# Routed rows fetched by indirect transfers instead of gathered on TensorE, and x added by VectorE instead of by an accumulating transfer

## The reference: what is computed

```
xn = layernorm(x)
s  = causal_attention(xn)                        # one head of width 256
for each token: two experts of eight are picked, with weights w (softmax, bias, groups)
flat_idx = the picked expert numbers themselves  # values 0 to 7
routed_in = xn[flat_idx] * w                     # so only tokens 0 to 7 are ever read
h   = silu(routed_in @ w1[e]) * (routed_in @ w3[e]) ; routed_out = h @ w2[e]
out = shared_ffn(xn); out[flat_idx] += routed_out    # only tokens 0 to 7 are written
x  + s * silu(out)
```

## Time and profile before

| what | value |
|---|---|
| time, median of 3 runs | 243.1 us (241.94 to 243.17) |
| time of the profiled execution | 242.11 us |
| span of the profiled execution | 240.4 us |
| mean granted TensorE clock | 0.999 of full speed |
| busy | PE 96%, DVE 74%, ACT 60%, POOL 24% |
| transfers | 19.45 MB, 81 GB/s over the span |

### The profile page before, as it was taken

The page is one execution under the profiler, slowest core; times in us unless marked ns, Lnnn a source line. Parts: engine busy times, 40 slices in busy tenths (PEclk is TensorE's granted clock), DMA queues, the critical chain, the costliest instruction groups (busy, mean ns, idle before and its releaser), DMA issues.

```text
span 240.4 us, 4667 instructions
## 1 busy us (share of the span) xinstructions
PE 230.6 (96%) x1553; PEld 204.5 (85%) x1553; DVE 177.1 (74%) x580; ACT 145.3 (60%) x390; POOL 57.5 (24%) x108
## 2 busy tenths in 40 slices
PE   6799999999999999999999999999999999999991
PEld 4789898998988989889899998898988879899760
DVE  3489658887987898878767976668586777769635
ACT  2445655755648557465575643877869686788711
POOL 3320721815508236072011000002020120202022
PEclk9999999999999999999999999999999999999999
DMA  6599420020200200000000000110845638375465
GB/s 183 189 323 307 138 87 3 5 84 4 87 4 0 87 3 1 1 3 0 0 3 0 1 3 3 48 40 11 203 73 155 115 108 169 78 189 86 140 121 180
DMA packets 18726, 19.45 MB, mean 81 GB/s; under 512 B 1032, under 2 KB 17680, under 8 KB 18704
## 3 DMA queue, kind: packets, MB, share of 16 engines
q1 hardware_dynamic: 15008, 15.50, 20.3%
q0 software_dynamic: 3696, 3.67, 10.0%
HBM read 14.95 MB, written 4.21 MB: 80 GB/s over the span
## 4 chain that ended last, share of the span: by engine, by line
PE 90%; DVE 4%; issue 1%; DMA 1%; ACT 1%; POOL 1%; DVEq 0%; ACTq 0%
PE bank L390 82%; PE bank L479 4%; PE bank L440 3%; DMA x_ring<-in_L_attn_x 1%; PE bank L412 1%; DVE x_ring L1349 1%; PE bank L431 1%; DVE bn L945 1%; DVE w L1343 1%; PE bank L547 1%; DVE xT_lo_all L936 1%; POOL rstd L307 0%; DVE arena L936 0%; DVE w L1265 0%; ACT w L885 0%
## 5 line engine op out<-in xcount | busy, mean ns | idle before, releaser
L390 PE MATMUL bank<-xT_hi_all,arena 128*128 128x512 f32 (+3 forms) x256 | 80.3, 369 | 0.0
L390 PE MATMUL bank<-arena 128*128 128x256 f32 (+2 forms) x560 | 75.9, 282 | 0.4 <-ACT attn_all L723 0.3
L390 PEld LDWEIGHTS bank<-arena 128*128 128x128 f32 (+1 forms) x560 | 71.0, 183 | 5.3 <-DVE arena L936 1.1
L723 ACT ACTIVATE arena<-bank 128x512 fp32r<-128x512 f32 (+4 forms) x84 | 36.3, 452 | 28.9 <-PE bank L390 27.4
L390 PEld LDWEIGHTS bank<-xT_hi_all,arena 128*128 128x128 f32 x256 | 47.0, 189 | 6.1 <-DVE arena L936 0.2
L936 DVE TENSOR_TENSOR arena<-bank,arena 128x264 fp32r<-128x264 f32 (+4 forms) x83 | 41.3, 507 | 14.3 <-ACT arena L723 14.1
L390 PE MATMUL bank<-xT_lo_all,arena 128*128 128x512 f32 (+3 forms) x128 | 45.8, 358 | 0.0
L376 POOL DMA_DIRECT2D x_ring<-in_L_attn_x x7 | 9.2, 1311 | 88.8 <-DVE x_ring L1284 88.8
L390 PEld LDWEIGHTS bank<-xT_lo_all,arena 128*128 128x128 f32 x128 | 24.2, 189 | 2.1
L723 ACT ACTIVATE attn_all<-bank,row_inv 128x256 f32<-128x256 f32 x32 | 15.2, 475 | 15.6 <-PE bank L390 14.7
L747 ACT ACTIVATE probs<-bank,neg_max 128x128 f32<-128x128 f32 (+3 forms) x32 | 17.0, 531 | 9.4 <-DVE neg_max L985 9.4
(11 more groups left out here) (125 smaller groups left out, 376.4 us busy)
## 6 DMA issues: line engine op xcount, KB each, us to landing
x_ring<-in_L_attn_x SPq DMA_DIRECT2D x8, 512.0 KB, 3.4
x_ring<-in_L_attn_x POOLq DMA_DIRECT2D x7, 512.0 KB, 5.8
out<-x_ring SPq DMA_DIRECT2D x7, 512.0 KB, 3.4
spread<-pairs SPq DMA_DIRECT2D x14, 128.0 KB, 3.4
w_sb<-in_L_ffn_w SPq DMA_DIRECT2D x1, 1024.0 KB, 10.9
raw_sw<-in_L_ffn_sw SPq DMA_DIRECT2D x3, 256.0 KB, 4.3
x_ring<-in_L_attn_x SPq DMA_DIRECT2D x2, 256.0 KB, 3.0
raw_qkv<-in_L_attn_WQ SPq DMA_DIRECT2D x1, 256.0 KB, 4.1
```

Of the source, the lines that this page charges most:

```text
L390: return nc.tensor.matmul(dst, lhsT, rhs, start=start, stop=stop, skip_group_check=True, **kw)
L723: return nc.scalar.activation(dst, src, ACT.Copy, scale=scale)
```

## The change

- Groups 1 to 7 (56 of the 64 tiles) no longer use `gather` and `one_hot`. The table A is written to DRAM once (64 rows of 512 bytes), and POOL issues 56 indirect transfers (`fetch_rows`), each of which fetches 128 rows of A by index into the SBUF space of `xn`. `silu_rows` reads from there. A group's buffer is fetched anew as soon as ACT has read it.
- The pair numbers' way through DRAM goes: `turn_pairs`, the ACT copy to `pair_T`, the store, and the 14 `spread` loads.
- x is loaded again by SP for all 8 batches (`reload_x`) into `x_ring`; the gate goes into `gate` instead, and DVE adds x in halves (`add_x`, 14 instructions). The 7 accumulating transfers on POOL go. `store` waits for its own landing before the next load.
- Added once: a copy of A and a transpose of it (`A_full`, `A_rows`), and the conversion of the pair numbers into indices (`pair_ids`).

```diff
 # SP
-            def load_pairs(i):
...
+            def reload_x(i):
+                sp.wait_ge(s["x_loaded"], 16 * (B + i - 1))
+                load_x(sequence(i), i)
             def store(i):
-                sp.wait_ge(s[f"summed{i % 2}"], 16 * (i // 2 + 1))
+                sp.wait_ge(s["summed"], 2 * (i + 1))
                 sp.dma_start(out_v[sequence(i), :, :, :], x_ring[:, i % 2, :, :]).then_inc(s[f"out_stored{i % 2}"], 16)
+                sp.wait_ge(s[f"out_stored{i % 2}"], 16 * (i // 2 + 1))
+            sp.wait_ge(s["xn_done"], B)
+            reload_x(0)
+            reload_x(1)
+            sp.wait_ge(s["a_rows_kept"], 1)
+            sp.dma_start(A_dram, A_rows[:, :]).then_inc(s["a_stored"], 16)
+            for i in range(B - 1):
                 store(i)
+                if i + 2 < B:
+                    reload_x(i + 2)
 # POOL
-            def add_x(i):
-                pool.wait_ge(s["gated"], 2 * (i + 1))
-                pool.dma_start(x_ring[:, i % 2, :, :], x_v[sequence(i), :, :, :], accum_op=ALU.add).then_inc(s[f"summed{i % 2}"], 16)
+            def fetch_rows(i, g):
+                if i > 1:
+                    pool.wait_ge(s["rows_silu"], RB * (i - 1) + RG * (g + 1))
+                for j in range(RG):
+                    r = i * RB + g * RG + j
+                    pool.indirect_dma_start(fetched[:, g, j, :], None, A_dram,
+                                            bass.IndirectOffsetOnAxis(pair_ids[:, r:r + 1], 0)).then_inc(s[f"rows_in{g}"], 16)
+            pool.wait_ge(s["x_turned"], C * B)
+            pool.wait_ge(s["a_stored"], 16)
+            pool.wait_ge(s["ids_ready"], 1)
+            fetch_rows(1, 0)
+            fetch_rows(1, 1)
+            for i in range(2, B):
+                fetch_rows(i, 0)
+                fetch_rows(i, 1)
 # PE, in each pass
-                gather(i, 0)
-                gather(i, 1)
 # PE, once
+            nc.tensor.transpose(x_bank[0][0:PAIRS, P:2 * P], A_full[:, :], ident[:, :]).then_inc(s["a_turned"], 1)
-            turn_pairs()
 # ACT
+            copy(A_full[:, :], x_bank[0][:, 0:PAIRS])
+            copy(A_rows[:, :], x_bank[0][0:PAIRS, P:2 * P]).then_inc(s["a_rows_kept"], 1)
-            copy(pair_T[:, :], acc_bank[0:NR, 3 * P:4 * P]).then_inc(s["pairs_kept"], 1)
             def silu_rows(i, g):
-                act.wait_ge(s["gathered"], 2 * i + g + 1)
+                if i > 0:
+                    act.wait_ge(s[f"rows_in{g}"], 16 * RG * i)
+                else:
+                    act.wait_ge(s["gathered"], g + 1)
             def silu_out(i, half):
...
-                to = gate if i == B - 1 else x_ring[:, i % 2, :, :]
-                nc.scalar.activation(to[:, 2 * half:2 * half + 2, :].rearrange("p t d -> p (t d)"), o_bank[:, :],
+                if i > 0:
+                    act.wait_ge(s["summed"], 2 * (i - 1) + half + 1)
+                nc.scalar.activation(gate[:, 2 * half:2 * half + 2, :].rearrange("p t d -> p (t d)"), o_bank[:, :],
                                      ACT.Silu).then_inc(s["gate_done"], 1)
 # DVE
+            def add_x(i, half):
+                dve.wait_ge(s["x_loaded"], 16 * (B + i))
+                dve.wait_ge(s["gated"], 2 * i + half + 1)
+                slot = x_ring[:, i % 2, 2 * half:2 * half + 2, :]
+                nc.vector.tensor_tensor(slot, slot, gate[:, 2 * half:2 * half + 2, :], ALU.add).then_inc(s["summed"], 1)
+            nc.vector.tensor_scalar(pair_ids[:, :], pair_rows[:, :], 8.0, None, ALU.add).then_inc(s["ids_ready"], 1)
             def step2(i):
-                one_hot(i, 0)
                 rows_low(i - 1, 1)
                 gate_attn(i - 1, 0).then_inc(s["gated"], 1)
-                one_hot(i, 1)
                 h_mult(i, 0)
+                add_x(i - 1, 0)
                 pair_one_hots(i, 0)
                 rows_low(i, 0)
                 h_mult(i, 1)
                 gate_attn(i - 1, 1).then_inc(s["gated"], 1)
                 h_low(i, 0)
                 pair_one_hots(i, 1)
                 h_low(i, 1)
+                add_x(i - 1, 1)
```

More of the change, by code:

```diff
@@ L148, in build @@
         pair_rows = sb("pair_rows", [P, NR], BF16)
-        pair_T = sb("pair_T", [NR, P], BF16)
-        spread = sb("spread", [P, 2, RG * P], BF16)
-        pairs_dram = nc.dram_tensor("pairs", [NR, P], BF16).ap()
+        pair_ids = sb("pair_ids", [P, NR], mybir.dt.uint32)
+        A_full = sb("A_full", [P, PAIRS])
+        A_rows = sb("A_rows", [PAIRS, P])
+        fetched = xn[:, :, :].rearrange("p t d -> p (t d)").rearrange("p (g r h) -> p g r h", g=2, r=RG)
+        A_dram = nc.dram_tensor("A_table", [PAIRS, H], F32).ap()
         gs = sb("gs", [P, NT, G])
@@ L371, in _ @@
             score(B - 1)
-            def add_x(i):
-                pool.wait_ge(s["gated"], 2 * (i + 1))
-                pool.dma_start(x_ring[:, i % 2, :, :], x_v[sequence(i), :, :, :], accum_op=ALU.add).then_inc(s[f"summed{i % 2}"], 16)
-            for i in range(B - 1):
-                add_x(i)
-            pool.wait_ge(s["x_loaded"], 16 * B)
+            def fetch_rows(i, g):
[13 more added lines that the diff above has]
+                fetch_rows(i, 1)
+            pool.wait_ge(s["x_loaded"], 16 * (2 * B - 1))
             pool.wait_ge(s["last_gated"], 1)
@@ L613, in shared_out, with spread_pairs @@
                 ins.then_inc(s["o_done"], 1)
-            def turn_pairs():
-                mm(acc_bank[0:NR, 3 * P:4 * P], pair_rows[:, :], ident_bf[:, :], True, True).then_inc(s["pairs_turned"], 1)
-            def spread_pairs(g):
+            def spread_pairs(i, g):
                 if g == 1:
-                    pe.wait_ge(s["one_hot_done"], g)
+                    pe.wait_ge(s["one_hot_done"], 1)
                 for j in range(RG):
                     r = g * RG + j
-                    ins = mm(bc_bank[:, j * P:(j + 1) * P], pair_rows[:, r:r + 1].to_broadcast([P, P]), ident_bf[:, :], True, True)
+                    ins = mm(bc_bank[:, j * P:(j + 1) * P], pair_rows[:, bass.ds(i * RB + r, 1)].to_broadcast([P, P]), ident_bf[:, :], True, True)
                 ins.then_inc(s["bc_done"], 1)
@@ L645, in _ @@
             pe.wait_ge(s["a_split"], 2)
-            nc.tensor.transpose(x_bank[0][:, 0:P], A_T[:, :].bitcast(F32), ident[:, :]).then_inc(s["a_turned"], 1)
+            nc.tensor.transpose(x_bank[0][:, 0:P], A_T[:, :].bitcast(F32), ident[:, :])
+            nc.tensor.transpose(x_bank[0][0:PAIRS, P:2 * P], A_full[:, :], ident[:, :]).then_inc(s["a_turned"], 1)
             table(1, 0)
@@ L865, in silu_rows @@
                     r = g * RG + j
-                    nc.scalar.activation(row_silu[:, g, j, :], g_bank[:, j * H:(j + 1) * H], ACT.Silu,
+                    rows = fetched[:, g, j, :] if i > 0 else g_bank[:, j * H:(j + 1) * H]
+                    nc.scalar.activation(row_silu[:, g, j, :], rows, ACT.Silu,
                                          scale=w_rows[:, bass.ds(i * RB + r, 1)]).then_inc(s["rows_silu"], 1)
@@ L1250, in one_hot @@
             def one_hot(i, g):
-                if i > 0:
-                    dve.wait_ge(s[f"spread{g}"], 16 * i)
-                    dve.wait_ge(s["gathered"], 2 * i + g - 1)
-                else:
-                    dve.wait_ge(s["bc_done"], g + 1)
-                ids = bc_bank[:, :] if i == 0 else spread[:, g, :]
-                nc.vector.tensor_scalar(one_hot_T[:, g, :], ids, pair_of_partition[:, 0:1], None,
+                dve.wait_ge(s["bc_done"], g + 1)
+                nc.vector.tensor_scalar(one_hot_T[:, g, :], bc_bank[:, :], pair_of_partition[:, 0:1], None,
                                         ALU.is_equal).then_inc(s["one_hot_done"], 1)
@@ L1334, in _ @@
             h_low(i, 1)
-            dve.wait_ge(s["x_loaded"], 16 * B)
+            add_x(i - 1, 1)
+            dve.wait_ge(s["x_loaded"], 16 * (2 * B - 1))
             def times_attn(n):
```

40 lines of the change are left out of this document (8 added, 32 removed).

## The result

The changed kernel takes 252.9 us (median of 4 runs, 250.67 to 253.9), the kernel before beside it 242.5 (241.47 to 243.17): a ratio of 1.0452, 95% interval 1.0394 to 1.0511. The forecast was 237.1. The profiled execution took 253.78 us, its span is 251.7.

The account below looks back on a forecast made before the run. PE, busy 96% of the span, was taken as the bound: 242.11 profiled, less 6.2 of gathers, plus 0.1 for the start, gave 236.0; with 1.0 up to the median, 237.1. Own range 236 to 239, full range 235.6 to 256.

Parts of the forecast that it names:

- POOL sets the pass: Rival: POOL's row of 48 indirect issues sets the time, 245.4 at c = 1.28, 256 at 1.50; chance 0.31.
- c: Time of one indirect issue on POOL, taken as 1.06 us; whole gain needs c below 1.10, 0.04 above that value.
- POOL, the unknown: Step estimating POOL's indirect issue between 0.35 and 1.75 us, taken as 1.06; eight a pass need 8.5 of 9.41 us.
- the prediction's own formula: Start of `silu_rows(7, 1)`: 163.05 (160.05 plus some 3 us of landing) plus 48 issues of c each; before, 222.22.
- all of the gain gone: Limit on POOL's issue time: at 1.23 us, (222.22 - 163.05) / 48, nothing of the 6.2 us gain is left.
- issues longer than 1.1: Sign listed under "Wrong": indirect issues on POOL would take longer than 1.1 us.
- those of `silu_rows` waiting and of passes over 9.6: Two signs listed under "Wrong": ACT's `silu_rows` waiting for a transfer, and a pass over 9.6 us.
- PE's saving: 56 gather matmuls leave PE at 0.11 us each: 0.88 a pass, 6.2 us over seven passes.
- The `add_x` on DVE at nothing: Two `add_x` a pass on DVE, 0.68 us each, stand where they cost PE nothing; uncovered, 1.2 a pass.
- x by SP's queue hidden: Store and reload of x on SP's queue take about 7 us, wanted about 13 us later: hidden, 5 us left.
- Issues on POOL hold up DVE: Rival: indirect issues and DVE's two-input work could not overlap, a pass would take 15 us, total 276; chance 0.07.
- The about 1 us: Skill page's overhead for emitting a transfer from GpSimd; by it POOL needs 8.0 us a pass, same sum.

Follow-up runs that it names:

- e_plain: Changed kernel with each of the 56 indirect transfers replaced by a plain POOL transfer of the same size, without indices (routed sums left out): 236.61 us, ratio 0.9781.
- e_nofetch: Changed kernel without its 56 indirect transfers, the silu working on what lies in the buffer: 235.18 us, ratio 0.9723 to the kernel before.
- e_xonly: Kernel before with only x's second load by SP and the DVE adds, gathers still on PE: 242.35 us, ratio 1.0033.
- e_half: Changed kernel with two of each four rows fetched, 28 of 56 indirect transfers: 235.49 us, ratio 0.9748 to the kernel before.
- e_mix4: Changed kernel with only group 1 of each pass fetched (28 transfers), group 0 gathered on PE as before, single buffers: 242.19 us, ratio 1.0032.
- e_mix6: Changed kernel with six of eight tiles of a pass fetched and two gathered on PE, single buffers: 242.02 us, ratio 0.9991 to the kernel before.
- e_after_2buf: Changed kernel with its fetch buffers doubled, nothing left out: 253.27 us, ratio 1.0424 to the kernel before.

## Why the prediction was wrong

**The direction was wrong; the rival "POOL sets the pass" came true** (0.31, beginning at c = 1.23; its range to 256 holds the result).

**The step that failed is "POOL, the unknown".** The duration of an issue, c = 1.06, was right (1.053). What was wrong is that I let the next issue begin where the last one ends, and priced 48 issues as 48 durations. What counts is start to start: 1.375 us. Two terms were missing. The gap of 0.30 ahead of every indirect issue (16.5 us for 54) was in no row of before, where POOL never issued two transfers in a row. And 0.11 of the 1.053 is waiting behind two-input instructions of DVE: an undisturbed issue takes 0.94. So my 1.06 was right by luck: I had put 0.81 on the transfer and 0.25 on the indices; a plain transfer of this size took 0.54 (e_plain), an indirect one 0.40 more, and the waits behind DVE make the 0.11. Nor were there 144 packets: the page after has 1792 for 56 transfers, 32 each. With 0.94 + 0.30 = 1.24 POOL would just have stood at the point I gave for "all of the gain gone", 1.23. Put in the prediction's own formula, 163.05 + 48 x 1.375 = 229.05 for `silu_rows(7, 1)`; it was 230.51, as the 48 issues began 0.3 later than I had put them, took 66.3 and not 66.0, and the landing behind the last took 3.8 and not 3.

**The price of the rival was too low.** By its formula (222.22 to 229.05, 6.8 late) the profiled execution comes to 248.9; it took 253.8. Of the 4.8 between, 1.5 are the still later `silu_rows(7, 1)`, 3.0 the tail and 0.4 lie outside the span. Of the tail 1.65 is clock: behind its holes PE ran the routed output at the lower level, which neither the formula nor the forecast held. That rival names the right engine and the right wait, but not the reason: its sign "issues longer than 1.1" didn't show (1.053), those of `silu_rows` waiting and of passes over 9.6 did.

**Right.** PE's saving: 6.2 worked out, 6.7 measured (e_nofetch: 242 x 0.0277, its interval 5.0 to 8.3), and 9.40 a pass in e_plain, where 9.41 was worked out. (The sum as written adds up to 237.0, not 237.1; nothing hangs on it.) The `add_x` on DVE at nothing, with 0.68 each, and x by SP's queue hidden: e_xonly. That the gain stands as long as POOL's issues fit into PE's pass: e_half, and the passes of e_mix4 and e_mix6.

**"Issues on POOL hold up DVE"**, the rival at 276, went the other way round: DVE's two-input instructions keep their 0.68, and it is POOL's issue that waits for them to end, mostly for 0.3 to 0.5 us. The page "SBUF — State Buffer" of the Trainium skill says under "Who interferes with whom" that a VectorE instruction with two SBUF inputs contends with a GpSimd instruction that reads SBUF, and calls the shared ports an exclusive lock. The trace agrees where DVE was first: the issue ends 0.81 to 0.82 after that instruction in 122 cases. Where the issue was first, it did not keep DVE out: 23 such instructions began during one and took 0.68 to 0.72. No run took the DVE instructions away, but the issues beside `h_mult` (46, all 0.94 to 0.95) and the plain ones of e_plain are what an issue does without that wait.

**The about 1 us** that the page "DMA: Bandwidth & Descriptors" of the Trainium skill gives under "Latency and other measured facts" as the overhead of emitting a transfer from GpSimd is near the 0.94 of an indirect issue and twice the 0.54 of a plain one. Neither is what paces a row of them: that is 0.56 for plain ones and 1.24 at least for indirect ones, from start to start.

## What to carry to other kernels

When a queue's own engine becomes the pacemaker, price its instructions from start to start, with whatever stands between two of them, and where no row shows two in a row, put that gap into the upper bound. If the forecast rests on being 0.04 us inside a limit, move less: half the tiles fetched, behind a doubled buffer, took 1% off, all of them cost 4.5%. And the longest holes of TensorE were paid twice, once as waiting and once as clock (2.67 us waited, then 1.7 lost on 16 matmuls); those up to 1.61 in the middle of the phase were paid once.

## What the runs showed of the hardware that I had not expected

- Two indirect transfers of 128 rows in a row on POOL have 0.30 us between them in which POOL neither works nor waits for anything that the profile shows; plain transfers of the same size have none.
- An indirect issue takes 0.94 us, a plain one of the same 128 rows 0.54.
- An indirect issue that begins during a DVE instruction with two SBUF inputs stands until that one has ended, and doesn't slow it: begun early in one it takes up to 1.45 us, and it ends 0.81 to 0.82 after it. Plain issues (0.53 to 0.54) don't wait.
- After a hole of 2.67 us a run of 16 matmuls took 3.78 us, its like 2.05 to 2.17; behind one of 3.11 us in e_after_2buf it took 2.54.
- Waits of 6 to 11 us on DVE and ACT beside rows of indirect issues, of which the last 4 to 7 have no cause in the rows, in three of the nine kernels that made such issues; their cause is open.
